# Expert passes of a graph network: the sums of two groups in one run of 48 products

## The chip, the cores and the metric

One core of a Trainium2 chip runs the whole program. The metric is the device time of one execution in microseconds (us), the median over the runs. The engines are named as in the profile: PE is TensorE (PEld its weight loads), DVE VectorE, ACT ScalarE, POOL GpSimd, SP SyncE.

## The reference, cut to what matters

Four graph layers follow one another on 6250 nodes and 106250 edges, which are sorted by their target. The change touches the second layer alone, a mixture of experts with three levels (N, H = 6250, 256):

```python
h = x @ W_in + b_in
for l in range(3):
    agg = segment_sum(h[src], dst, num_segments=N) / deg
    logits = concatenate([h, agg], -1) @ router_W[l] + router_b[l]
    vals, idx = top_k(logits, 2); gates = softmax(vals)
    gate_dense = zeros_like(logits).at[rows, idx].set(gates)
    weak = relu(einsum('nh,ehf->nef', agg, weak_W[l]) + weak_b[l])           # 4 experts
    sh = relu(einsum('nh,ehf->nef', agg, strong_W1[l]) + strong_b1[l])       # 4 experts
    strong = einsum('nef,efh->neh', sh, strong_W2[l]) + strong_b2[l]
    moe = einsum('ne,neh->nh', gate_dense, concatenate([weak, strong], 1))
    h = h + sigmoid(h @ conf_W[l] + conf_b[l]) * moe
return h @ W_out + b_out
```

## The kernel before

Each level is one pass over the edges (`edge_pass` with `width == H`), and the experts of a block of 128 nodes are computed in the same pass, between the sums of the edges.

**The edges.** 128 edges are a tile, four tiles a group (`GROUP`), four groups a turn of the ring (`RING` = 16 slots in SBUF). POOL fills a slot with an indirect DMA of the 128 source rows (L546); each row holds h cut into three bf16 parts, so a tile is 128 x 768 bf16. POOL may gather into slot k of the next turn once `tiles_done` says that the slot's products are made (L544). DVE writes one-hot matrices for eight tiles at a time (L622), PE makes six products of 64 columns per tile (L696) that add up a group's sums in a PSUM bank, 24 per group, and DVE adds the group's sums into `acc` at the group's window (L662 to L669). There are two such banks: the products of group n wait until group n-2 has been added (`added`), and the addition of group n waits for `tiles_done`. A pass has 208 groups. `tiles_done` rises by four with the last product of a group; POOL, DVE and PE's partners read it.

**The blocks.** A pass is written out as 49 steps (`STEP_GROUPS`: 6, then eleven times 4, 4, 4, 5, then 4, 4, 4, 3 groups). Each step also does one block of nodes. The block's work is cut into pieces with a due place from 0 to 15, which `over` spreads over the tiles of the step, on each engine in program order: first the tile's own work, then the pieces that are due. Before the change PE runs a group's 24 products at the group's fourth tile. In a step of four groups PE's order is:

```text
down2 down3 | h_t weak0 | G0 | logits weak1 up0 up1 | G1 | down0 up2 | G2 | down1 up3 | G3
```

`down2` and `down3` (L1159) belong to the block before (`late_pe`), `h_t` (L1175), `weak` (L1184), `logits` (L1210), `up` (L1198) and `down` to the block itself (`on_pe`). `agg` (L1097, DVE) is the first piece of a block: it reads `acc` after all sums of the step before, so it waits for the last addition; `weak0` waits for `agg`. `logits` waits for ACT's copy of `h_t` (L1056), `up1` for DVE's `biased0` (L1106), which waits for `weak0`. `down0` waits for `relu0` (ACT, L1082), which stands behind `relu_w1` (L1062), which waits for `biased1`. `down3` of the next step waits for `relu3` and `mix5` (L1087).

DVE's order in the same step is: one-hots, `agg`, `mix6`, `next_row` and its cuts, addition of G0, `biased0` and the routing, addition of G1, six mixes, one-hots, three mixes, addition of G2, `mix5`, addition of G3.

In a step of five groups the pieces lie a little further apart: PE's order is `down2 down3 | G0 | h_t weak0 logits weak1 | G1 | up0 up1 | G2 | down0 up2 down1 | G3 | up3 | G4`.

Of the kernel before, what the change touches and what calls it, by code (L numbers as in the profile page):

```python
# [7 lines left out]
D = 128  # L8
H = 256
# [5 lines left out]
GROUP = 4  # L15
WIN = 64
RING = 16
HALF = RING // 2
GROUPS = RING // GROUP
# [4 lines left out]
STEP_GROUPS = (6,) + PERIOD * PERIODS + (4, 4, 4, 3)  # L24
STEPS = len(STEP_GROUPS)
FIRST_GROUP = [sum(STEP_GROUPS[:i]) for i in range(STEPS + 1)]
assert FIRST_GROUP[STEPS] == TURNS * GROUPS
ROW = GROUP * P
SETS = -(-E // (ROW * P))
TCOLS = SETS * P * GROUP  # L30
# [4 lines left out]
SPARE = SPARE_BLOCK * P  # L35
# [32 lines left out]
ALU = mybir.AluOpType  # L68
# [82 lines left out]
def gnn_kernel(nc, t, out):  # L151
    ctx = ExitStack()
    with ctx:
# [8 lines left out]
        gathered = [ctx.enter_context(nc.semaphore(f"gathered{k}")) for k in range(RING)]  # L162
# [32 lines left out]
        acc = sb("acc", [P, 2, NPAD])  # L195
# [5 lines left out]
        win = sb("win", [1, GCOLS], I32)  # L201
# [225 lines left out]
        def edge_pass(table, width, work, edge_net=None, prologue=None):  # L427
# [11 lines left out]
            with ExitStack() as tmp:  # L439
# [24 lines left out]
                def programs(block, sems, loop):  # L464
# [143 lines left out]
                    @block.vector  # L608
                    def _(dve):
                        if loop == "blocks" and not edge_net:  # L610
                            first_round()

                        def one_hots(i, h):

                            dve.wait_ge(tiles_done, i * RING + HALF * (h + 1))
                            cols = rel[:, bass.ds(i * RING + h * HALF, HALF)].unsqueeze(2).to_broadcast([P, HALF, WIN])
                            places = iota_row[:, :].unsqueeze(1).to_broadcast([P, HALF, WIN])
                            if edge_net:
                                dve.wait_ge(sem[f"rel_loaded{h}"], i * 16 + 16)
                                nc.vector.tensor_scalar(onehot_t[:, h, :], relb[:, h, :], iota_col[0:WIN, 0:1], None,  # L620
                                                        ALU.is_equal)
                            nc.vector.tensor_tensor(onehot[:, h, :, :], places, cols, ALU.is_equal).then_inc(onehot_ready, 1)  # L622

                        def dots(i, g):

                            n = i * (2 * GROUPS) + 2 * g
                            k = g * GROUP
                            dve.wait_ge(sem["z_done"], i * GROUPS + (g + 1))
                            nc.vector.tensor_tensor(hidden[:, :, :], zt[:, g % 2, :, :], ring[:, k:k + GROUP, 0:D],
                                                    ALU.subtract).then_inc(sem["net_own"], 1)  # L630
                            dve.wait_ge(sem["net_own"], n + 1)
                            nc.vector.scalar_tensor_tensor(
                                out=hidden[:, :, :], in0=hidden[:, :, :], scalar=0.0,
                                in1=w2.unsqueeze(1).to_broadcast([P, GROUP, D]), op0=ALU.max,
                                op1=ALU.mult).then_inc(sem["net_own"], 1)
                            dve.wait_ge(sem["net_own"], n + 2)
                            nc.vector.tensor_reduce(dot[:, g % 2, :], hidden[:, :, :], AX.X,
                                                    ALU.add).then_inc(sem["dot_done"], 1)

                        def tile(i, k, ahead=True):  # L640
                            g, q = divmod(k, GROUP)
                            if edge_net and q == 0:

                                dve.wait_ge(sem["weight_done"], i * GROUPS + (g + 1))
                                dve.wait_ge(tiles_done, i * RING + GROUP * (g + 3))
                                j = g * GROUP % HALF
                                nc.vector.tensor_tensor(onehot_w[:, g % 2, :, :], onehot[:, g // 2, j:j + GROUP, :],  # L647
                                                        weight[:, g % 2, :].unsqueeze(2).to_broadcast([P, GROUP, WIN]),
                                                        ALU.mult).then_inc(sem["weighted"], 1)
                            if q == 0 and g % 2 == 0:  # L650

                                one_hots(i + g // 2, 1 - g // 2)
                            if q < GROUP - 1:
                                return
                            if edge_net and (ahead or g < GROUPS - 1):

                                dots(i + (g + 1) // GROUPS, (g + 1) % GROUPS)
                            if edge_net:
                                if i * GROUPS + g >= 1:
                                    add_sums(i * GROUPS + g - 1)  # L660
                                return
                            w = dve.value_load(win[0:1, bass.ds(i * GROUPS + g, 1)], min_val=0, max_val=SPARE)  # L662
                            dve.wait_ge(tiles_done, i * RING + (GROUP * (g + 1) + RING))

                            dve.wait_ge(added, i * GROUPS + (g + 2))
                            nc.vector.tensor_tensor(  # L666
                                acc[:, 0:n_sums, bass.ds(w, WIN)], acc[:, 0:n_sums, bass.ds(w, WIN)],
                                sums[:, g % 2, 0:n_sums * WIN].rearrange("p (a j) -> p a j", j=WIN),
                                ALU.add).then_inc(added, 1)  # L669

                        def add_sums(n):

                            w = dve.value_load(win[0:1, bass.ds(n, 1)], min_val=0, max_val=SPARE)
                            dve.wait_ge(sem["turned"], n + 1)
                            dve.wait_ge(added, n + 2)
                            nc.vector.tensor_tensor(acc[0:1, 1, bass.ds(w, WIN)], acc[0:1, 1, bass.ds(w, WIN)],
                                                    sums[0:1, n % 2, WIN:2 * WIN], ALU.add)
                            nc.vector.tensor_tensor(acc[:, 0, bass.ds(w, WIN)], acc[:, 0, bass.ds(w, WIN)],
                                                    sums[:, n % 2, 0:WIN], ALU.add).then_inc(added, 1)

                        if loop == "edges":
                            dve.sem_inc(added, 2)
                            one_hots(0, 0)
                        if edge_net:
                            if loop == "edges":
                                nc.vector.memset(ring[:, :, YH:YH + 1], 1.0)
                                dots(0, 0)
                            over(dve, tile, lambda i, k: tile(i, k, ahead=False), lambda: add_sums(LAST_GROUP))
                        else:
                            over(dve, tile)  # L690

                    @block.tensor
                    def _(pe):
                        def tile_sum(ap, lhs, rhs, first, last=False):

                            return nc.tensor.matmul(ap, lhs, rhs, start=first, stop=last, skip_group_check=True)  # L696
# [45 lines left out]

                        def tile(i, k):
                            g, q = divmod(k, GROUP)
                            if k % HALF == 0:
                                pe.wait_ge(onehot_ready, i * 2 + (k // HALF + 1))
                            if q == 0:

                                pe.wait_ge(added, i * GROUPS + (g + 1))
                            burst = width == H  # L750
                            if burst and q < GROUP - 1:
                                return
                            for j in range(k - q if burst else k, k + 1):
                                pe.wait_ge(gathered[j], i * 16 + 16)
                                hot = onehot[:, g // 2, j % HALF, :]
                                for a in range(width // D):
                                    for c in range(PARTS):
                                        lo = c * width + a * D
                                        last = tile_sum(sums[:, g % 2, a * WIN:(a + 1) * WIN], ring[:, j, lo:lo + D],
                                                        hot, j % GROUP == 0 and a == 0 and c == 0, j % GROUP == GROUP - 1)  # L760
                            if q == GROUP - 1:
                                last.then_inc(tiles_done, GROUP)

                        if loop == "edges":
                            pe.sem_inc(tiles_done, RING)
# [1900 lines left out]
```

## Time and profile before

| | us |
|---|---|
| median of three runs | 8308.41 (8306.09 to 8310.05) |
| the profiled execution | 8296.74 |
| its span, first to last instruction | 8294.9 |
| first start of a sum product of the expert passes, last start | 1084.2, 5499.2 |
| granted TensorE clock over the span | 0.846 |

Busy shares over the whole span: PE 82%, PEld 60%, DVE 48%, ACT 25%, POOL 40%. The clock has two levels, shown as 0.5 and 1.0 of 2.4 GHz; a figure between is a mean over time. In a timeline row the first number is the start in us, the second its length, and the brackets at the end give the idle time of that engine just before and what ended it by the profile. Rows that follow one another with one line and shape are merged (x24).

### The profile page before, as it was taken

Reading aid. Unit: us, or ns where it says so; the run is one execution under the profiler, and the core shown is the slowest. Engines: PE = TensorE matmul, PEld = TensorE weight load, DVE = VectorE, ACT = ScalarE, POOL = GpSimd, SP = SyncE. Lnnn points to the kernel's source line nnn. Section 1 sums busy time; section 2 is a strip of 40 time slices with the busy share of each in tenths; the row PEclk is TensorE's granted clock in tenths of the full one; section 3 lists DMA queues with packets and bytes.
Section 4 is the critical chain, followed back from the end, with each engine's and each line's share of the span. In section 5 each row is a group of like instructions: output and inputs, shape, how many; then the busy total and the mean of one; then the engine's idle time right before and its main releaser. Section 6 shows DMA issues by size and latency. Waiting matters only on the chain. (4 is left out here: it accounts for less than half of the span.)

```text
span 8294.9 us, 149947 instructions
## 1 busy us (share of the span) xinstructions
PE 6806.2 (82%) x51092; PEld 4987.8 (60%) x51092; DVE 3941.9 (48%) x11483; ACT 2108.0 (25%) x6166; POOL 3355.4 (40%) x3406
## 2 busy tenths in 40 slices
PE   3999858888886888888688888867677676989899
PEld 1555546777775776777577777755555553545455
DVE  7777634444443444444355554546666662112111
ACT  3555412222221222222233333322222221000000
POOL 0000055555554555555455555536666661000000
PEclk6999979999997999999899999985555557999999
DMA  5344355454544444455444444434444445656565
GB/s 149 110 147 117 124 151 143 141 143 142 146 138 138 139 141 137 140 145 142 134 141 141 137 139 138 138 89 124 127 125 128 125 125 186 198 171 196 175 203 162
DMA packets 714970, 1188.63 MB, mean 143 GB/s; under 512 B 258881, under 2 KB 512997, under 8 KB 712162
## 3 DMA queue, kind: packets, MB, share of 16 engines
q0 software_dynamic: 200640, 601.97, 26.2%
q1 hardware_dynamic: 466786, 447.42, 18.0%
q10 hardware_dynamic: 46784, 129.65, 4.4%
q8 instruction: 411, 6.73, 0.3%
q14 instruction: 349, 2.86, 0.1%
HBM read 993.57 MB, written 185.20 MB: 142 GB/s over the span
## 5 line engine op out<-in xcount | busy, mean ns | idle before, releaser
L546 POOL DMA_INDIRECT ring<-parts,src_idx x2496 | 2453.7, 983 | 1948.1 <-PE sums L696 749.9
L1198 PEld LDWEIGHTS hid<-agg,big 128*128 128x128 f32 x9408 | 1157.1, 197 | 124.6 <-issue 88.1
L1198 PE MATMUL hid<-agg,big 128*128 128x128 f32 x9408 | 1184.7, 281 | 45.8 <-issue 27.3
L2346 PE MATMUL agg_ps<-sheet,big 128*128 128x448 f16 x6174 | 1193.6, 353 | 34.7 <-DMA sheet<-adj 34.7
L1159 PE MATMUL y<-big,strong 128*128 128x256 f32 x4704 | 1143.2, 390 | 37.3 <-issue 27.9
L546 POOL DMA_INDIRECT ring<-rows_yh,src_idx x832 | 839.5, 1009 | 556.8 <-issue 326.3
L1159 PEld LDWEIGHTS y<-big,strong 128*128 128x128 f32 x4704 | 868.8, 192 | 155.7 <-issue 50.1
L666 DVE TENSOR_TENSOR acc<-acc,sums 128x128 f32 x624 | 180.0, 289 | 1634.4 <-DMA acc<-in_edge_type 1116.1
L2346 PEld LDWEIGHTS agg_ps<-sheet,big 128*128 128x128 bf16 x6174 | 605.0, 99 | 581.7 <-DMA sheet<-adj 37.4
L1082 ACT ACTIVATE strong<-hid,s_b 128x128 f32<-128x128 f32 x2352 | 668.2, 369 | 916.5 <-PE hid L1198 625.4
L696 PE MATMUL sums<-onehot,ring 128*128 128x64 bf16 x14976 | 627.7, 196 | 320.5 <-issue 254.5
L696 PEld LDWEIGHTS sums<-onehot,ring 128*128 128x128 bf16 x14976 | 570.0, 100 | 480.3 <-issue 440.6
L1184 PE MATMUL hid<-big,agg 128*128 128x512 f32 x1176 | 764.8, 784 | 68.0 <-DVE agg L1097 65.8
L739 PE MATMUL by_target<-ring,onehot_w 128*64 128x129 f32 x1664 | 409.1, 427 | 133.7 <-DVE onehot_w L647 105.8
L1087 DVE SCALAR_TENSOR_TENSOR row<-y,gate,row 128x256 f32<-128x256 f32 x588 | 282.8, 481 | 376.5 <-DMA adj<-big 278.7
L739 PEld LDWEIGHTS by_target<-ring,onehot_w 128*64 128x64 f32 x1664 | 328.4, 223 | 178.8 <-issue 176.3
L1931 PE MATMUL counts_ps<-hot_col,hot 128*128 128x392 bf16 (+3 forms) x1960 | 348.2, 299 | 101.2 <-DVE hot_col L1790 96.7
L1184 PEld LDWEIGHTS hid<-big,agg 128*128 128x128 f32 x1176 | 257.5, 242 | 278.2 <-issue 204.8
L1062 ACT ACTIVATE weak<-weak 128x512 f32<-128x512 f32 x294 | 184.9, 629 | 822.1 <-DVE weak L1106 685.3
L1762 POOL MEMSET acc<- 128x10976 f32 x1 | 9.2, 9245 | 940.1 <-PE deg_ps L1931 940.1
L2458 DVE SCALAR_TENSOR_TENSOR agg<-agg_ps,counts_hold,acc 128x448 f32<-128x448 f32 x42 | 28.7, 684 | 723.2 <-PE agg_ps L2346 723.2
L2402 POOL MEMSET acc<- 128x448 f32 (+1 forms) x28 | 13.4, 480 | 872.9 <-DVE agg L2458 872.9
(370 smaller groups left out, 8529.5 us busy)
## 6 DMA issues: line engine op xcount, KB each, us to landing
sheet<-adj SPq DMA_DIRECT2D x294, 784.0 KB, 4.2
ring<-parts,src_idx POOLq DMA_INDIRECT x2496
adj<-big ACTq DMA_DIRECT2D x7, 5488.0 KB
adj<-acc ACTq DMA_DIRECT2D x7, 5488.0 KB
hp<-parts SPq DMA_DIRECT2D x147, 192.0 KB
relb<-rel_rows ACTq DMA_DIRECT2D x106, 256.0 KB
parts<-cut SPq DMA_DIRECT2D x99, 192.0 KB, 3.2
h<-rows SPq DMA_DIRECT2D x147, 128.0 KB
```

The lines of the kernel that those rows point to most:

```text
L546: nc.gpsimd.indirect_dma_start(ring[:, k, 0:YH] if edge_net else ring[:, k, :], None, table, bass.IndirectOffsetOnAxis(ap=src_idx[:, i * R ...
L666: nc.vector.tensor_tensor(acc[:, 0:n_sums, bass.ds(w, WIN)], acc[:, 0:n_sums, bass.ds(w, WIN)], sums[:, g % 2, 0:n_sums * WIN].rearrange(" ...
L696: return nc.tensor.matmul(ap, lhs, rhs, start=first, stop=last, skip_group_check=True)
L739: last = nc.tensor.matmul(by_target[:, g % 2, 0:D + 1], onehot_w[:, g % 2, j, :], ring[:, g * GROUP + j, D:YH + 1], start=(j == 0), stop=( ...
L1062: m.done(f"relu_w{q}", nc.scalar.activation(both, both, ACT.Relu))
L1082: ins = nc.scalar.activation(s["strong"][:, e % 2, j, :], p["hid"][:, bank_at, j * P:(j + 1) * P], ACT.Relu, bias=self.w["s1_b"][:, e, j:j ...
L1087: m.done(name, nc.vector.scalar_tensor_tensor(out=out, in0=expert, scalar=self.b[0]["gate"][:, e:e + 1], in1=so_far, op0=ALU.mult, op1=ALU ...
L1159: ins = nc.tensor.matmul(y, s["strong"][:, e % 2, k, :], w["s2"][:, k, e, :], start=(k == 0), stop=(k == 3))
L1184: ins = nc.tensor.matmul(hid, s["agg"][:, k, :], w["weak"][:, k, 2 * q:2 * q + 2, :].rearrange("p e f -> p (e f)"), start=(k == 0), stop=( ...
L1198: ins = nc.tensor.matmul(p["hid"][:, bank_at, j * P:(j + 1) * P], w["s1"][:, k, e, j * P:(j + 1) * P], s["agg"][:, k, :], start=(k == 0), ...
L1931: return nc.tensor.matmul(ap, lhs, rhs, start=first, stop=last, skip_group_check=True)
L2346: last = nc.tensor.matmul(ps[:, g % 2, 0:HALF_COLS], now[:, b, c, :], sheet[:, k, s * HALF_COLS:(s + 1) * HALF_COLS], start=(b == 0 and c ...
```

## The change

In the expert passes the groups of a step are paired: (0, 1), (2, 3), and the last of an odd number alone. PE does nothing at the first group of a pair; at the last tile of the second it makes both groups' products, 48 in one run, each group with its own waits and its own rise of `tiles_done`. DVE does both additions at the same place. Where the second group of a pair is an even one, the one-hots that used to be made at its first tile are made behind the two additions. PE's order in a step of four groups is now `down2 down3 h_t weak0 logits weak1 up0 up1 | G0 G1 | down0 up2 down1 up3 | G2 G3`; in a step of five, `down2 down3 h_t weak0 logits weak1 | G0 G1 | up0 up1 down0 up2 down1 | G2 G3 | up3 | G4`.

```diff
+PAIRS = [tuple(range(FIRST_GROUP[i] + g, FIRST_GROUP[i] + min(g + 2, STEP_GROUPS[i])))
+         for i in range(STEPS) for g in range(0, STEP_GROUPS[i], 2)]
+PAIR_AT_END = {pair[-1]: pair for pair in PAIRS}
+SECOND = {pair[1] for pair in PAIRS if len(pair) > 1}
...
-                            if q == 0 and g % 2 == 0:
-
+                            n = i * GROUPS + g
+                            if g % 2 == 0 and q == (GROUP - 1 if not edge_net and n in SECOND else 0):
+                                if q:
+                                    pair_sums(n)
                                 one_hots(i + g // 2, 1 - g // 2)
+                                if q:
+                                    return
...
-                            w = dve.value_load(win[0:1, bass.ds(i * GROUPS + g, 1)], min_val=0, max_val=SPARE)
-                            dve.wait_ge(tiles_done, i * RING + (GROUP * (g + 1) + RING))
-
-                            dve.wait_ge(added, i * GROUPS + (g + 2))
-                            nc.vector.tensor_tensor(
-                                acc[:, 0:n_sums, bass.ds(w, WIN)], acc[:, 0:n_sums, bass.ds(w, WIN)],
-                                sums[:, g % 2, 0:n_sums * WIN].rearrange("p (a j) -> p a j", j=WIN),
-                                ALU.add).then_inc(added, 1)
+                            pair_sums(n)
+
+                        def pair_sums(end):
+
+
+                            for n in PAIR_AT_END.get(end, ()):
+                                w = dve.value_load(win[0:1, bass.ds(n, 1)], min_val=0, max_val=SPARE)
+                                dve.wait_ge(tiles_done, GROUP * (n + 1) + RING)
+
+                                dve.wait_ge(added, n + 2)
+                                nc.vector.tensor_tensor(
+                                    acc[:, 0:n_sums, bass.ds(w, WIN)], acc[:, 0:n_sums, bass.ds(w, WIN)],
+                                    sums[:, n % 2, 0:n_sums * WIN].rearrange("p (a j) -> p a j", j=WIN),
+                                    ALU.add).then_inc(added, 1)
...
-                            if k % HALF == 0:
-                                pe.wait_ge(onehot_ready, i * 2 + (k // HALF + 1))
-                            if q == 0:
-
-                                pe.wait_ge(added, i * GROUPS + (g + 1))
-                            burst = width == H
-                            if burst and q < GROUP - 1:
+                            if q < GROUP - 1:
                                 return
-                            for j in range(k - q if burst else k, k + 1):
-                                pe.wait_ge(gathered[j], i * 16 + 16)
+                            for n in PAIR_AT_END.get(i * GROUPS + g, ()):
+                                group_sums(n)
+
+                        def group_sums(n):
+
+
+                            pe.wait_ge(onehot_ready, n // 2 + 1)
+                            pe.wait_ge(added, n + 1)
+                            g = n % GROUPS
+                            for q in range(GROUP):
+                                j = g * GROUP + q
+                                pe.wait_ge(gathered[j], n // GROUPS * 16 + 16)
                                 hot = onehot[:, g // 2, j % HALF, :]
                                 for a in range(width // D):
                                     for c in range(PARTS):
                                         lo = c * width + a * D
-                                        last = tile_sum(sums[:, g % 2, a * WIN:(a + 1) * WIN], ring[:, j, lo:lo + D],
-                                                        hot, j % GROUP == 0 and a == 0 and c == 0, j % GROUP == GROUP - 1)
-                            if q == GROUP - 1:
-                                last.then_inc(tiles_done, GROUP)
+                                        last = tile_sum(sums[:, n % 2, a * WIN:(a + 1) * WIN], ring[:, j, lo:lo + D],
+                                                        hot, q == 0 and a == 0 and c == 0, q == GROUP - 1)
+                            last.then_inc(tiles_done, GROUP)
```

## Rows read from the trace of the kernel before

**Rows 1.** Windows, passes 1 and 3: length, busy time per engine, PE clock, DMA share.

```profile
1084.00:2498.00 1414.00, 1208.08 (x10645) 988.51 (x10646) 636.87 (x1889) 328.86 (x1057) 819.75 (x830) 0.91 0.51 146
4037.00:5500.00 1463.00, 1237.76 (x11043) 1016.82 (x11043) 714.93 (x2354) 497.61 (x1338) 799.15 (x823) 0.91 0.49 140
```

**Rows 2.** Page, costliest groups: count, busy us, mean ns, idle before, releaser.

```profile
L666 DVE TENSOR_TENSOR acc<-acc,sums 128x128 f32 x624 | 180.0, 289 | 1634.4 <-DMA acc<-in_edge_type 1116.1
L696 PE MATMUL sums<-onehot,ring 128*128 128x64 bf16 x14976 | 627.7, 196 | 320.5 <-issue 254.5
```

**Rows 3.** Timeline of PE, one step from its last-but-one group on.

```profile
1643.93 0.86 PE L696 MATMUL sums<-onehot,ring 128*128 128x64 bf16 x24
1644.63 3.70 PE L1159 MATMUL y<-big,strong 128*128 128x256 f32 x16
1648.17 0.50 PE L1175 MATMUL misc<-ident,hp 128*128 128x128 bf16 x6
1650.71 1.98 PE L1184 MATMUL hid<-big,agg 128*128 128x512 f32 x4 [2.04 <-DVE agg L1097]
...
1653.23 0.59 PE L1210 MATMUL misc<-router,ht 128*128 128x9 f32 x4
...
1654.12 1.96 PE L1184 MATMUL hid<-big,agg 128*128 128x512 f32 x4
1655.92 3.73 PE L1198 MATMUL hid<-agg,big 128*128 128x128 f32 x32
1659.49 0.86 PE L696 MATMUL sums<-onehot,ring 128*128 128x64 bf16 x24
```

**Rows 4.** Timeline of DVE, the additions around the same place.

```profile
1642.87 0.29 DVE L666 TENSOR_TENSOR acc<-acc,sums 128x128 f32 x1 [1.15 <-DMA acc<-in_edge_type]
...
1649.29 0.29 DVE L666 TENSOR_TENSOR acc<-acc,sums 128x128 f32 x1 [5.74 <-DMA acc<-in_edge_type]
...
1650.23 0.42 DVE L1097 TENSOR_TENSOR agg<-acc,rdeg 128x256 f32<-128x256 f32 x1
```

**Rows 5.** Timeline of POOL: first gathers of two runs of four in sequence.

```profile
1643.51 0.95 POOL L546 DMA_INDIRECT ring<-parts,src_idx  x1 [1.15 <-DMA acc<-in_edge_type]
...
1649.93 1.07 POOL L546 DMA_INDIRECT ring<-parts,src_idx  x1 [1.71 <-DMA acc<-in_edge_type]
```

**Rows 6.** Timeline of POOL: first gather of a run of eight, first of the next.

```profile
1704.80 1.07 POOL L546 DMA_INDIRECT ring<-parts,src_idx  x1 [1.62 <-PE sums L696]
...
1717.09 1.06 POOL L546 DMA_INDIRECT ring<-parts,src_idx  x1 [2.42 <-DMA acc<-in_edge_type]
```

**Rows 7.** Waits of POOL, 1100 to 5500: us in total, times, longest.

```profile
POOL ring L546 <- PE sums L696: 749.6, 243, 6.8
...
POOL ring L546 <- DMA acc<-in_edge_type: 441.5, 262, 3.7
```

**Rows 8.** Timeline of POOL and PE: a group's products late in a run of eight.

```profile
2149.30 0.95 POOL L546 DMA_INDIRECT ring<-parts,src_idx  x1 [2.15 <-DMA acc<-in_edge_type]
...
2149.37 0.86 PE L696 MATMUL sums<-onehot,ring 128*128 128x64 bf16 x24
...
2156.66 0.28 PE L696 MATMUL sums<-onehot,ring 128*128 128x64 bf16 x4
...
2160.69 0.72 PE L696 MATMUL sums<-onehot,ring 128*128 128x64 bf16 x16 [0.51 <-issue]
2161.22 2.06 PE L1198 MATMUL hid<-agg,big 128*128 128x128 f32 x8
```

**Rows 9.** Timeline of POOL, PE and ACT: `h_t` in a run of eight.

```profile
1730.25 1.06 POOL L546 DMA_INDIRECT ring<-parts,src_idx  x1 [1.63 <-DMA acc<-in_edge_type]
...
1733.96 0.50 PE L1175 MATMUL misc<-ident,hp 128*128 128x128 bf16 x6
...
1741.67 0.37 ACT L1056 COPY ht<-misc 128x256 f32<-128x256 f32 x1 [7.26 <-DMA h_in<-rows]
...
1742.10 1.02 PE L1210 MATMUL misc<-router,ht 128*128 128x9 f32 x4 [3.82 <-ACT ht L1056]
```

## The prediction

> **What bounds the kernel now.** I read the passes' windows first. Pass 1 takes 1414 us, of which PE is busy 1208 and idle 206: with 49 steps that is 28.9 us a step, 24.7 busy and 4.2 idle. Pass 3 has the same picture, 1463 with 225 idle; the granted clock is 0.91 in both, so part of the busy time is work at half speed [rows 1]. The groups of the page say what the change moves: 624 additions and 14976 products of 64 columns, 208 groups in each of three passes. DVE's 1634 us of idle time ahead of the additions costs nothing in itself, but it is put down to a DMA of long ago, so something else ends it [rows 2].
>
> The timeline of a clean step gives the work at full clock, from start to start: 16 `down` products 3.54 us, `h_t` and its copy's cover about 0.4, `logits` 0.89, one `weak` 1.80, the 32 products of two `up` 3.57, a group's sum 0.70 [rows 3]. A step of four groups is 32 `down` 7.1, `h_t` 0.4, two `weak` 3.6, `logits` 0.9, 64 `up` 7.1, four sums 2.8: 21.9, say 22.1 with the seams. So of 28.9 us 2.6 are half clock (24.7 less 22.1) and 4.2 idle.
>
> Then the waits. The group of 1643.93 ends at 1644.79, and DVE, which stands at its addition with nothing before it, adds at 1649.29 only, 4.5 us later. `agg` follows at 1650.23, and PE loses 2.04 us before `weak` [rows 3, 4]. In that time POOL issues four gathers: first at 1643.51, and the next run's first at 1649.93 [rows 5]. The addition comes when POOL has finished its run: **what PE reports while POOL issues gathers becomes visible late**, often only after the run. One run of four and the pause behind it takes 6.42 us (1649.93 less 1643.51); where two groups are ready, POOL issues eight in one run, 12.29 us from first to first [rows 6]. POOL waited for a group 505 times (243 and 262) for 624 groups, so some 119 groups joined a run already going [rows 7]. Four such cycles are 25.7 us a step: PE's chain and POOL's chain are both near the bound, and each stall feeds the other.
>
> **The change part by part.** Additions, products, one-hots and gathers are as many as before [rows 2]; the order alone changes.
>
> *POOL.* Both groups of a pair become ready 0.70 us apart, and nearly always before POOL's run has got going, so nearly every run is one of eight. A pair costs POOL 12.29 instead of 2 x 6.42 = 12.84 us: 0.55 us less, 104 pairs x 3 passes = 172 us if POOL's chain alone set the time. It is the lower bound of the change.
>
> *PE, behind the pair that ends a step.* `down2`, `down3` and `h_t` end about 4 us after the pair, `weak0` about 5.4. `weak0`'s report falls into the run of eight. A case shows what that means: run from 1730.25, `h_t` ends at 1734.46, 4.2 us into it, and ACT copies it at 1741.67, 11.4 us into it; PE's `logits` stand 3.82 us [rows 9]. Here `weak0` is late in the same way: `biased0` can't start before +11.4, `up1` not before +12.2. PE's own order is there at 5.4 + 0.9 + 1.8 + 1.8 = 9.9. Loss: 2.3 to 2.6 us. Before, additions of G0 stood ahead of `biased0` as well, and the loss was part of the 4.2.
>
> *PE, behind the pair in the middle.* `down0`, `up2`, `down1`, `up3` take 1.77 + 1.78 + 1.77 + 1.78 = 7.1 us, then G2 and G3 start 7.1 us into a run of eight. The rows hold the same place: run from 2149.30, 24 products start at 2156.66, 7.4 us into it. Four pass, then single ones, and 16 at once from 2160.69; the next work starts at 2161.22. 4.56 us for 0.70 [rows 8]. The first group of the pair meets this, the second comes at full pace: 3.9 us. Below, the loss is 0 if only the late report and not PE itself is slowed; above, 2 x 3.9. I take 3.9, which is a row's.
>
> *The half clock.* After that stretch eight `up` products take 2.06 us [rows 8], against 3.73 for 32 [rows 3]: half speed. There are two long stops a step now where there were up to four short ones. Between nothing and twice the present 2.6 us a step I take 1.9.
>
> The Trainium skill ("TensorE: Matmul & The Clock Gate", section "HAM oscillation — how this bites in real kernels") says that a pause which recurs in each round of a loop makes every round start at half clock. The trace agrees in the row just named; by the rule alone the loss would be the upper end, 5.2 us a step, and the sum 485 us higher.
>
> *DVE.* The second addition stands 1.15 + 0.29 us behind the first (the register load ahead of an addition is in the 1.15 [rows 4]), so `agg` moves by up to 1.4 us. The 3.54 us of `down` and `h_t` cover it [rows 3]; without them it is 1.4 x 147 steps = 206 us. The one-hots that move behind two additions, 0.7 us, have the 7 us of work between two pairs as cover.
>
> *ACT.* `logits` has no group ahead of it, but the 1.8 us of `weak0` cover ACT's copy of 0.37 [rows 9]; `relu0` comes behind `relu_w1` and `biased1`, which the late `biased0` moves to about +15, just where the middle pair ends: 0 to 0.6 us.
>
> *The gathers.* G0's slots come free some 6 us later than now and G2's 3.6. They are needed a step later, over 20 us, and filled in 5 to 10 us: nothing. The fifth group of a long step uses slots that G0 of the same step frees; 12 us of work lie between, four gathers take 5. Its own report falls 2.7 us into a run of eight and can hang until +11.4: up to 5 us in 11 steps a pass, which I leave to the upper end.
>
> **The sum.** A mean step: 22.1 work + 2.6 + 3.9 idle + 1.9 half clock = 30.5 us, against 28.9: 1.6 more, x 147 = 235 us. 8296.7 + 235 = 8532 for the profiled execution; the median of the runs lies 11.7 above that one: **8545 us**, 2.8% slower.
>
> **The rivals.**
>
> *POOL's chain is the bound, and fewer runs help: faster.* For it: 25.7 us a step at POOL against 22.1 at PE, and PE's 2.04 us before `weak` ends with POOL's run [rows 3 to 5]. Against it: the pass has 28.9 a step, so something beyond POOL's cycle costs 3.2. It gives 8308 - 172 = 8136 us. Chance 0.31.
>
> *`h_t` is caught too: slower by much.* In the forecast it ends about 4.0 us into the run; the case with 4.2 was held to 11.4 [rows 9]. If a slow pair delays `down2`, it is caught in every other step or more. Price: 3.8 us of stop and 1.2 of half clock behind it. It decides from an `h_t` that ends later than about 4.1 us into a run. In half of the steps: 5.0 x 73 = 367 on top, 8910 us. Chance 0.18.
>
> *Reports are not held by the run, the additions are merely late for another cause: no change.* The Trainium skill ("Perfetto Trace Analysis", section "Tensor Engine Instruction (MATMUL, LD_WEIGHTS)") has the semaphore update pushed when PSUM has acknowledged the writes, which would be at the group's end. The trace differs by 4.5 us [rows 4]. If reports were prompt after a pair, the order of the pieces would change nothing that PE waits for: 8308. Chance 0.08.
>
> The forecast has 0.43.
>
> **How the numbers follow.** Less than 0.2%, 17 us, can't be told from no change here. Faster: 0.31. Same: 0.08. Slower: 0.43 + 0.18 = 0.61. The range reaches from a little below the fast rival, 8120, to 8900, about where the second rival has half its weight; that leaves some 0.1 on either side. The forecast's own range, with the burst's loss from 2 to 5 us and the clock's from 1 to 3, is 8310 to 8850.
>
> **What would show it.** In the timeline of POOL nearly all runs have eight gathers, and its waits for groups fall from 505 to about 330. The first group of the middle pair takes over 4 us from its first product to its last, with single products about 0.7 us apart; the second takes 0.7. `up1` is released by `biased0` 12 us after the run's start. PE's idle share in the pass windows rises from 0.15 to above 0.2. The prediction is wrong if the products of a pair run through at 33 ns each although POOL is in a run of eight, if the additions follow a pair within half a us, or if PE's idle time in the pass falls. The granted clock of the windows tells how much of a difference is half clock: I expect 0.90 to 0.93.

## The result, and the profile of the changed kernel

The changed kernel takes 8754.7 us (8710.0 to 8771.7, four runs), the kernel before 8307.3 beside it: a ratio of 1.0528, with a 95% interval of 1.0492 to 1.0564. It is 447 us slower, where 238 were forecast. All ratios below are to the kernel before on the same chip, whose median moved between 8257 and 8311 us from chip to chip.

The windows of the three expert passes say where the loss lies. The rows that answer to those of before ([rows 1] for the first pass) are these, of the changed kernel. The columns are length, then busy time and count for PE, PE's weight loads, DVE, ACT and POOL, granted clock, DMA share and GB/s:

```profile
1084.00:2599.00 1515.00, 1224.26 (x10630) 1012.08 (x10631) 651.48 (x1889) 323.95 (x1057) 806.72 (x827) 0.89 0.47 135
2599.00:4163.00 1564.00, 1245.97 (x10777) 1030.12 (x10776) 667.03 (x1937) 330.60 (x1079) 811.38 (x832) 0.89 0.46 133
4163.00:5938.00 1775.00, 1350.74 (x11200) 1101.92 (x11199) 741.59 (x2403) 504.75 (x1360) 804.03 (x832) 0.86 0.41 118
```

and for passes 2 and 3 of the kernel before, from the last group of one pass to the last of the next:

```profile
2498.00:3983.00 1485.00, 1245.75 (x10774) 1017.71 (x10774) 654.09 (x1936) 334.70 (x1078) 822.55 (x832) 0.90 0.49 140
3983.00:5500.00 1517.00, 1263.09 (x11198) 1037.00 (x11197) 730.65 (x2401) 504.41 (x1360) 808.44 (x832) 0.91 0.49 138
```

Length less before's length: +101, +79, +258, in all 438 of the 455 us by which the profiled spans differ. The gain in PE's busy time is 16, 0 and 88, so the rest is idle PE: +85, +79 and +170. The first two passes lose what was forecast (1.6 us x 49 steps = 78 each), or a little more; the third loses more than three times as much. PE's idle share of the three is 0.19, 0.20 and 0.24.

**Inside a pass the loss is not spread over the steps.** These windows of the changed kernel are four steps in a row of pass 1, each up to the end of its last group. The first is a long step of five groups, the second the step behind it, and then come two ordinary ones:

```profile
1709.89:1742.96 33.07, 26.87 (x240) 22.11 (x240) 14.37 (x41) 6.19 (x21) 17.19 (x18) 0.86 0.44 124
1742.96:1780.63 37.67, 26.56 (x216) 20.50 (x216) 12.97 (x38) 7.20 (x24) 17.24 (x18) 0.86 0.42 119
1780.63:1808.68 28.05, 24.71 (x216) 20.75 (x216) 13.28 (x39) 6.84 (x23) 15.94 (x17) 0.93 0.49 140
1808.68:1836.37 27.69, 24.20 (x216) 20.62 (x216) 13.58 (x40) 6.68 (x22) 16.11 (x17) 0.93 0.49 141
```

The same four of the kernel before:

```profile
1670.49:1704.57 34.08, 28.57 (x239) 22.02 (x238) 13.21 (x40) 6.60 (x22) 18.67 (x20) 0.85 0.48 138
1704.57:1730.58 26.01, 23.59 (x216) 19.39 (x216) 13.57 (x41) 7.00 (x25) 15.98 (x17) 1.00 0.52 144
1730.58:1760.74 30.16, 25.37 (x216) 20.92 (x216) 13.56 (x40) 6.91 (x23) 16.59 (x17) 0.89 0.48 137
1760.74:1788.81 28.07, 24.63 (x215) 20.07 (x215) 13.20 (x39) 6.91 (x23) 15.50 (x16) 0.94 0.48 139
```

The two ordinary steps are together 2.5 us shorter in this example, the long one 1.0 shorter, and the step behind it is 11.7 us longer. Over all steps of passes 1 and 2, each from the end of the last group before it to the end of its own last, the 48 ordinary ones (four groups, and four in the step before) take 28.0 us on average (27.9 before), the 22 long ones 31.8 (33.2) and the 22 behind a long one 36.2 (27.1). The last kind loses 22 x 9.1 = 200 us; the long steps give 31 back. The timeline of the step behind the long one shows why. First PE and then DVE of the changed kernel (start, length, engine, line, operation, what went out and in, and in brackets the idle time before it):

```profile
1742.10 0.86 PE L712 MATMUL sums<-onehot,ring 128*128 128x64 bf16 x24
1742.80 3.70 PE L1178 MATMUL y<-big,strong 128*128 128x256 f32 x16
...
1752.79 3.78 PE L1203 MATMUL hid<-big,agg 128*128 128x512 f32 x4 [5.62 <-DVE agg L1116]
1758.40 0.61 PE L1229 MATMUL misc<-router,ht 128*128 128x9 f32 x4 [1.83 <-ACT ht L1075]
```

```profile
1740.65 0.29 DVE L682 TENSOR_TENSOR acc<-acc,sums 128x128 f32 x1 [0.54 <-PE sums L712]
...
1751.40 0.29 DVE L682 TENSOR_TENSOR acc<-acc,sums 128x128 f32 x1 [9.47 <-DMA acc<-in_edge_type]
1752.31 0.42 DVE L1116 TENSOR_TENSOR agg<-acc,rdeg 128x256 f32<-128x256 f32 x1 [0.62 <-DVE acc L682]
```

and POOL's run of eight under it, its first gather and the first of the next run:

```profile
1740.47 0.94 POOL L552 DMA_INDIRECT ring<-parts,src_idx  x1 [8.33 <-PE sums L712]
...
1752.05 0.94 POOL L552 DMA_INDIRECT ring<-parts,src_idx  x1 [1.88 <-DMA acc<-in_edge_type]
```

The long step's fifth group stands alone behind the pair and 16 `up` products. It ends at 1742.96, 2.5 us into a run of eight that the pair started. Its addition comes at 1751.40, 10.9 us into that run; `agg` waits for the addition, and PE's `weak` stands 5.62 us for `agg`. `logits` stand 1.83 more for ACT's copy of `h_t`, and the products behind these stops run at half clock (four `weak` in 3.78 us, 1.98 in [rows 3]).

**The ordinary step** has the forecast's slow group, though. It is G2, in the step's second pair (G2 G3), which the prediction and some expectations call the middle pair. PE of the changed kernel, this pair and the `down` products of the next step:

```profile
1676.56 0.42 PE L712 MATMUL sums<-onehot,ring 128*128 128x64 bf16 x9
...
1679.33 0.19 PE L712 MATMUL sums<-onehot,ring 128*128 128x64 bf16 x1 [1.22 <-issue]
1680.04 0.19 PE L712 MATMUL sums<-onehot,ring 128*128 128x64 bf16 x1 [0.52 <-issue]
1680.74 1.51 PE L712 MATMUL sums<-onehot,ring 128*128 128x64 bf16 x35 [0.52 <-issue]
1682.07 5.05 PE L1178 MATMUL y<-big,strong 128*128 128x256 f32 x16
```

Single products 0.7 us apart, 5.5 us for the pair's 48 instead of 1.4, then `down` at half speed for a while (5.05 us against 3.70 in [rows 3]). Over the 72 four-group steps of passes 1 and 2, G2 takes 4.9 us (median) where a group alone takes 0.86, and G3 1.35.

### The profile page after: what moved, and what is told of

Its sections match the earlier page's. It is cut to its first block and busy times, and to the rows that moved or that the text cites. A ratio compares the mean times of both kernels' runs of the same rounds, so it can differ in the third digit from the quotient of the medians.

```text
span 8749.9 us, 150208 instructions
## 1 busy us (share of the span) xinstructions
PE 6913.1 (79%) x51092; PEld 5088.9 (58%) x51092; DVE 3980.3 (45%) x11483; ACT 2099.1 (24%) x6166; POOL 3329.8 (38%) x3406
## 5 line engine op out<-in xcount | busy, mean ns | idle before, releaser
L552 POOL DMA_INDIRECT ring<-parts,src_idx x2496 | 2427.4, 972 | 2422.0 <-PE sums L712 1535.8
L1178 PE MATMUL y<-big,strong 128*128 128x256 f32 x4704 | 1281.7, 426 | 129.3 <-ACT strong L1101 74.8
L1217 PE MATMUL hid<-agg,big 128*128 128x128 f32 x9408 | 1163.7, 279 | 21.3 <-issue 21.2
L1178 PEld LDWEIGHTS y<-big,strong 128*128 128x128 f32 x4704 | 976.4, 216 | 289.7 <-ACT strong L1101 81.6
L712 PE MATMUL sums<-onehot,ring 128*128 128x64 bf16 x14976 | 651.0, 203 | 408.5 <-issue 337.2
L1203 PE MATMUL hid<-big,agg 128*128 128x512 f32 x1176 | 701.5, 727 | 120.6 <-DVE agg L1116 115.4
L1203 PEld LDWEIGHTS hid<-big,agg 128*128 128x128 f32 x1176 | 238.1, 225 | 311.6 <-issue 186.1
L1125 DVE TENSOR_TENSOR weak<-hid,weak_b 128x512 f32<-128x512 f32 x294 | 202.5, 689 | 446.3 <-PE hid L1203 200.0
L724 PE MATMUL zt<-ywin,onehot_t 64*128 64x128 bf16 x2496 | 345.4, 306 | 18.4 <-DMA ring<-rows_yh,src_idx 12.8
L2477 DVE SCALAR_TENSOR_TENSOR agg<-agg_ps,counts_hold,acc 128x448 f32<-128x448 f32 x42 | 28.7, 684 | 724.0 <-PE agg_ps L2365 724.0
```

The source lines that it names most:

```text
L552: nc.gpsimd.indirect_dma_start(ring[:, k, 0:YH] if edge_net else ring[:, k, :], None, table, bass.IndirectOffsetOnAxis(ap=src_idx[:, i * R ...
L724: last = nc.tensor.matmul(zt[:, g % 2, q, :], onehot_t[:, g // 2, (k % HALF) * P:(k % HALF + 1) * P], ywin[:, g, c * D:(c + 1) * D], start ...
L1125: m.done(f"biased{q}", nc.vector.tensor_tensor(s["weak"][:, 2 * q:2 * q + 2, :], p["hid"][:, q, :].rearrange("p (e f) -> p e f", f=H), sel ...
L1178: ins = nc.tensor.matmul(y, s["strong"][:, e % 2, k, :], w["s2"][:, k, e, :], start=(k == 0), stop=(k == 3))
L1203: ins = nc.tensor.matmul(hid, s["agg"][:, k, :], w["weak"][:, k, 2 * q:2 * q + 2, :].rearrange("p e f -> p (e f)"), start=(k == 0), stop=( ...
L1217: ins = nc.tensor.matmul(p["hid"][:, bank_at, j * P:(j + 1) * P], w["s1"][:, k, e, j * P:(j + 1) * P], s["agg"][:, k, :], start=(k == 0), ...
```

## The experiments

Twelve kernels ran. Each part starts with the edit.

**The fifth group.** Only the cuts of the long step change:

```diff
-PAIRS = [... for g in range(0, STEP_GROUPS[i], 2)]        # G0 G1 | G2 G3 | G4
+CUTS = {5: (0, 2, 3)}                                     # G0 G1 | G2 | G3 G4
+PAIRS = [... from each of CUTS.get(STEP_GROUPS[i], range(0, STEP_GROUPS[i], 2)) to the next]
```

> The fifth group of a long step is no longer alone behind a pair: the pairs of a five-group step are (G0 G1), G2, (G3 G4), so the pair stands at the step's end and G4's report is made together with G3's. The trace of the changed kernel shows 33 steps that follow a five-group step, mean 35.6, 36.7 and 38.7 us in the three passes, where the other four-group steps take 28, 28 and 34. Theory (G4's report falls some 2.5 us into a run of eight and hangs until its end, so the addition, agg and weak0 come late): these 33 steps fall to the others' length, 11 x (7.6 + 8.8 + 4.6) = 230 us less, about 8520. Rival (pairs cost in every step alike, the long step only shows where two slips add up): the time stays within 60 us of 8755. Second rival (the lone G2 now has a report of its own that is held in the same way): half is given back, 8640.

Measured: 8513.8 us, 1.0262 (1.0230 to 1.0295), against 8520 expected. Its pass windows:

```profile
1084.00:2504.00 1420.00, 1198.76 (x10635) 1004.45 (x10635) 651.46 (x1888) 323.79 (x1055) 812.07 (x828) 0.91 0.51 145
2504.00:3966.00 1462.00, 1223.17 (x10781) 1022.06 (x10776) 667.31 (x1936) 329.80 (x1080) 817.23 (x832) 0.90 0.50 142
3966.00:5699.00 1733.00, 1348.50 (x11203) 1110.23 (x11200) 739.26 (x2401) 507.45 (x1363) 808.71 (x832) 0.87 0.42 120
```

Passes 1 and 2 are back at the length of before (+6 and -23 us), although their steps still have pairs and slow middle groups. The third keeps +216.

**The third pass.** As that kernel, but the third pass takes its groups singly:

```diff
+single = bool(getattr(work, "last", None))
+pair_at_end = {n: (n,) for n in range(TURNS * GROUPS)} if single else PAIR_AT_END
```

> As the kernel with the long step's pairs at its end (8513.8 us), but the third expert pass takes its groups singly, as the kernel before does. In the trace of that kernel passes 1 and 2 take 1413 and 1404 us, against 1404 and 1429 before, and the third 1675 against 1462. Theory (in the third pass each step has more trips between PE and other engines, agg ahead of h_t, and the transposes and products of the output, and each of their reports hangs in the run of eight): the third pass falls back to about 1465, 8300 in all. Rival (the third pass suffers from its start or from what the passes before leave, not from its own pairs): it stays above 1600, 8450 or more.

Measured: 8235.8 us, 0.9975 (0.9965 to 0.9986); on the scale of the other chip 8311 x 0.9975 = 8290, against 8300 expected. The third pass takes 1513 us with 248 idle. So two edits, made one after the other, take the whole loss away: some 240 us (8754.7 less 8513.8) go with the long step's lone group and some 225 (8513.8 less 8290) with the pairs of the third pass. What is left is 0.25% faster than the kernel before.

**Without the gathers.** Both kernels with POOL's loop over turns cut to the first one in the expert passes, so that the first sixteen tiles are summed again and again:

```diff
-for i in turns(pool, 0, TURNS):
+for i in turns(pool, 0, TURNS if edge_net else 1):
...
-pe.wait_ge(gathered[j], n // GROUPS * 16 + 16)             # before the change: i * 16 + 16
+pe.wait_ge(gathered[j], 16)
```

> The changed kernel without the gathers of turns 1 to 51 in the three expert passes: only the first sixteen tiles are gathered and their rows are summed again and again, so POOL is idle in the passes; PE's order, waits on additions, one-hots and block work are as in the changed kernel. Theory (all that the pairs cost comes from POOL's runs of gathers, through held reports and a slowed PE): a step is PE's own work, 22.1 us or a little more, at the granted clock 1.0, about 147 x 6.5 = 950 us under the kernel before, near 7350, and the same as the kernel before with the same omission within 20 us. Rival (the order itself costs, the later agg and one-hots): over 100 us more than the kernel before with the same omission.

> The kernel before without the gathers of turns 1 to 51 in the three expert passes (first sixteen tiles summed again and again). Theory: the same as the changed kernel with this omission, near 7350, within 20 us. Rival: over 100 us less than that one. If it is far above 7350, PE's own chain and not POOL's runs holds most of a step's 28.9 us.

Measured: 7307.1 us with the changed order (0.8797, 0.8779 to 0.8814) and 7316.4 with the order of before (0.8807, 0.8790 to 0.8823). A stretch of 100 us in pass 1, first of the changed order, then of the other:

```profile
1500.00:1600.00 100.00, 100.00 (x989) 86.27 (x988) 61.69 (x179) 31.41 (x100) 0.00 (x0) 1.00 0.13 38
```

```profile
1500.00:1600.00 100.00, 100.00 (x997) 86.31 (x996) 59.98 (x174) 30.79 (x99) 0.00 (x0) 1.00 0.12 36
```

In this stretch PE never stops and has full clock. Pass 1 with its start takes 1085 us for 49 steps, 22.1 a step, the forecast's figure, and PE is idle for 19 to 22 us of it. So nearly all of PE's waits in both kernels, and nearly all of the half clock, need the gathers; the order of the groups makes 9 us of difference without them. What the omission can't tell is whether POOL's issuing or the DMA traffic that goes with it (a DMA share of 0.51 in pass 1, 0.13 here) does the harm. The mean traffic alone does not decide: the kernel with pauses below has a DMA share of 0.50 over the passes, the slower changed kernel 0.45.

**Runs of eight without pairs.** The kernel before, with one wait of POOL changed:

```diff
-pool.wait_ge(tiles_done, i * RING + (k + 1))
+pool.wait_ge(tiles_done, i * RING + (k // 8 * 8 + 8))      # expert passes
```

> The kernel before with one wait of POOL changed: in the expert passes POOL starts on a group's slots only when both groups of a half ring are summed, so every run has eight gathers, while PE, DVE and ACT keep their order with single groups. Theory (the loss is made by runs of eight, not by PE's products standing in pairs): slower than before by 2 to 6%, 8420 to 8750, with h_t, weak0 or a group wherever they fall between 3 and 11 us into a run. Rival (a run of eight harms only what stands right behind a pair in PE's order): within 1% of before, 8310 or a little less, since a pair of groups costs POOL 12.3 instead of 12.8 us.

Measured: 8941.8 us, 1.0811 (1.0793 to 1.0830): more than the theory's upper end. PE's order, additions and one-hots are those of before, so long runs of gathers alone make more than the changed kernel's loss; its pairs in PE's order are, if anything, the better fit to such runs. POOL also starts later here, but rows that come too late are not the cause: PE's waits for gathered rows in the passes are 86 us, before 64, of a loss of 676.

**Pauses in POOL.** If an unbroken run does the harm, a short stop should help. Behind each fourth gather POOL writes a small tile of its own, each memset waiting for the one before:

```diff
+if not edge_net and k % GROUP == GROUP - 1:
+    for r in range(PAUSES):                    # 2; also 1 and 3
+        pool.wait_ge(sem["paused"], (i * RING + k) // GROUP * PAUSES + r)
+        nc.gpsimd.memset(pause[:, :], 0.0).then_inc(sem["paused"], 1)   # 128 x 320
```

On the changed kernel, with two:

> The changed kernel with a pause of two small memsets (about 0.8 us together) on POOL behind each fourth gather of the expert passes: a run of eight becomes two of four with a short pause. Theory (PE's reports and PE's own issue recover when POOL stops issuing gathers for a moment): the first group of the middle pair takes 1 to 2 us instead of 5, G4's report comes after the first four gathers, and the time falls by 150 to 350 us, to 8400 to 8600. Rival (what counts is how many gathers POOL has issued or how much is in flight, not that the run is unbroken): the middle pair still takes 5 us and the pauses add to POOL's chain, 8755 or up to 100 more.

Measured: 8267.3 us, 0.9959 (0.9941 to 0.9976), 487 less than the changed kernel and less than the 8400 to 8600 expected. But the reason given is only half right. The products of a second pair of this kernel:

```profile
1752.66 1.18 PE L721 MATMUL sums<-onehot,ring 128*128 128x64 bf16 x35
...
1754.76 0.28 PE L721 MATMUL sums<-onehot,ring 128*128 128x64 bf16 x4 [0.50 <-issue]
1756.20 0.28 PE L721 MATMUL sums<-onehot,ring 128*128 128x64 bf16 x4 [1.16 <-issue]
```

The slow stretch has moved from the pair's first group to its second; it is not gone (G3 takes over 2 us in 63 of 72 steps, G2 in none). The waits of PE over the passes tell what is gone. Waited for, us in total, times, longest; first the changed kernel, then the one with pauses:

```profile
PE sums L712 <- issue: 337.2, 453, 5.1
PE hid L1203 <- DVE agg L1116: 115.4, 21, 12.0
PE misc L1229 <- ACT ht L1075: 92.6, 31, 10.1
PE misc L1194 <- DVE agg L1116: 91.7, 13, 10.8
PE y L1178 <- ACT strong L1101: 74.8, 23, 4.9
```

```profile
PE sums L721 <- issue: 330.1, 517, 2.8
...
PE hid L1212 <- DVE agg L1125: 44.8, 21, 4.6
PE misc L1238 <- ACT ht L1084: 39.2, 20, 4.3
...
PE misc L1203 <- DVE agg L1125: 15.5, 7, 6.1
```

Waits for the answer of another engine fall from 375 us in these rows to 100, and those for `strong` are no longer among the large ones; PE's slow issue in the sums stays (337 and 330). Idle PE falls by 348 us in the passes, and its busy time by 149, at a granted clock of 0.92 against 0.88.

With two memsets and the long step's pair at its end:

> The long step's pairs at its end, and POOL's pause of two memsets (0.8 us) behind each fourth gather. Alone the one gave 8514 and the other 8267. Theory (both take away the same thing in the long step, a report that hangs to the end of a run of eight; the pause takes the third pass's loss too): less than the sum, 40 to 80 us below 8267, because the steps behind a long one still take 30 us there against 26.5: about 8200. Rival (with pauses the place of the pairs is indifferent): 8267 within 20.

Measured: 8080.4 us, 0.9785 (0.9764 to 0.9807), better than expected (8200 is 0.987). With one memset in place of two, else as the last:

> As the kernel with the long step's pairs at its end and pauses, but a pause of one memset (about 0.4 us) instead of two. Theory (any stop lets the held reports through): as with two, or 20 to 50 us less, because a four costs POOL 0.4 us less: 8170 to 8200. Rival (the stop must be long enough for what waits): part of the loss comes back, the middle pair takes over 2 us and the third pass over 1500: 8300.

Measured: 8333.8 us, 1.0100 (1.0075 to 1.0124). That is the rival's side: one stop of 0.4 us takes part of the loss only (1.0262 without a stop, 0.9785 with two). From the second pass's last group to the third's it takes 1610 us, against 1446 with two.

With two memsets, the long step's pair at its end and the third pass in single groups:

> Pairs with the long step's pair at its end in passes 1 and 2, single groups in the third, and the pause of two memsets behind each fourth gather. Passes of 1343 and 1345 us were measured with pairs and pauses, 1318 and 1323 with single groups and pauses; the third takes 1391 with pairs and 1418 single. Theory (the three passes add up): 8080 + 27 = about 8105 on the chip where those gave 8080 and 8058, 0.981 of before. Rival (the order makes a pass faster or slower than its own pairs say): over 30 us from that.

Measured: 8093.7 us, 0.9798 (0.9781 to 0.9814), as expected (0.981). With the long step's pair at its end, pairs in all passes, and the pause between the two fours of a pair only:

> As the kernel with pauses and the long step's pair at its end (0.9785 of before), but POOL pauses only between the two fours of a pair, not behind the second, where it mostly waits for PE anyway. Theory (only an unbroken run of eight costs, a pause at its end gives nothing): the same as with all pauses, or up to 40 us less where POOL goes straight on: 0.974 to 0.979. Rival (the pause behind the second four lets reports through also): 0.985 or more.

Measured: 8161.1 us, 0.9873 (0.9856 to 0.9889): the rival's figure. The stop behind the pair's second four counts too.

On the kernel before, whose groups are single:

> The kernel before with POOL's pause of two memsets (0.8 us) behind each fourth gather. It has 114 runs of eight in the passes, with 3.2 us of idle PE in each against 0.4 in a run of four. Theory (unbroken runs cost): the runs of eight lose most of that, some 250 us, while runs of four pay up to 0.8 where POOL's chain holds the step: 8100 to 8250. Rival (before's bound is POOL's chain, 4 x 6.42 a step; each pause adds to it): 4 x 0.4 to 0.8 more in a step, 8400 to 8700.

Measured: 8057.9 us, 0.9757 (0.9733 to 0.9780); on the scale of the other chip 8311 x 0.9757 = 8109, at the theory's lower bound. With three memsets:

> The kernel before with a pause of three memsets (1.2 us) behind each fourth gather. One memset (0.4) gave little in the paired kernel, two (0.8) gave most. Theory (a stop has to be long enough for what PE holds back; beyond that it only adds to POOL's chain): with the need met by two, 0.4 us x 4 a step more on POOL, slower than with two: 0.980 to 0.995 of before. Rival (what PE holds back is not all out after two): faster than 0.9757 of before.

Measured: 8037.6 us, 0.9723 (0.9706 to 0.9739): the rival's side, though the two intervals touch. It is the fastest of all, faster than both kernels. But the passes tell it apart: 1351, 1399 and 1417 us, with two memsets 1327, 1378 and 1475. In the first two the third memset costs 24 and 21 us, as the theory had it; all that it gains is in the third pass. Its four gathers and pause take 6.57 us from first to first, as these two rows of POOL say:

```profile
1705.17 1.22 POOL L550 DMA_INDIRECT ring<-parts,src_idx  x1 [0.36 <-issue]
...
1711.74 1.08 POOL L550 DMA_INDIRECT ring<-parts,src_idx  x1 [0.36 <-issue]
```

208 x 6.57 = 1367 us, about the length of a pass (1351 for the first): POOL's chain is now near the bound. PE's waits say the same, where gathered rows take the first place:

```profile
PE sums L705 <- DMA ring<-parts,src_idx: 312.3, 309, 10.7
PE misc L1184 <- DVE agg L1106: 55.8, 34, 3.6
PE sums L705 <- issue: 49.0, 90, 2.1
```

## Why the prediction was right in sign and short in size

*What bounds the kernel: shown.* PE's own work is 22.1 us a step; the remaining 6.8 need POOL's gathers (the pair of runs without them). The rival in which POOL's chain is the bound and fewer runs help is refuted by the kernel with runs of eight alone, 8% slower. The rival in which no report is held is refuted by the addition that comes 8.4 us behind its group.

*Nearly all runs have eight: right.* POOL's waits for groups fall from 505 to 320 (288 and 32 in the passes), against 330 forecast.

*The late `biased0`, 2.6 us a step: wrong, it costs nothing.* PE's waits in the passes have no row for `up1` behind `biased0` any more (14 waits, 17.6 us before). In an ordinary step of passes 1 and 2 `h_t` ends 5.5 us into a run of eight (from 1654.43) and is copied 0.3 us later, and `biased0` follows 8.0 us into the run, where 11.4 was forecast. PE, ACT and DVE:

```profile
1659.40 0.50 PE L1194 MATMUL misc<-ident,hp 128*128 128x128 bf16 x6
```

```profile
1660.20 0.37 ACT L1075 COPY ht<-misc 128x256 f32<-128x256 f32 x1 [3.57 <-PE misc L1194]
```

```profile
1662.43 0.69 DVE L1125 TENSOR_TENSOR weak<-hid,weak_b 128x512 f32<-128x512 f32 x1 [0.53 <-PE hid L1203]
```

The forecast took over [rows 9]: held from 4.1 us on. In the kernel before that was nearly a rule: of 52 `h_t` that ended 4 us or more into a run of eight, ACT waited over 2 us for 50. With pairs it is 16 of 89 in passes 1 and 2, and 26 of 33 in the third. Why some reports in the second half of a run get through these runs do not settle.

*The additions behind a pair: a sign of being wrong, and it came.* The prediction called itself wrong if the additions follow a pair within half a us. In the four-group steps of passes 1 and 2 the last addition starts 0.2 us (median) behind the end of the step's last group, and within half a us in 59 of 72; before it was 3.1 us. Here the group ends at 1780.63:

```profile
1780.83 0.29 DVE L682 TENSOR_TENSOR acc<-acc,sums 128x128 f32 x1 [0.53 <-PE sums L712]
```

So PE's wait for `agg`, 0.7 us in a mean ordinary step before, is gone from the ordinary steps of these passes and stands behind the long ones (4.0 and 4.3 us a step there).

*The slow first group of the second pair, 3.9 us: right.* It costs 4.1 us in the step shown (5.5 less 1.4), and an ordinary step of passes 1 and 2 has 3.5 us of idle PE, 3.2 of them in the sums. With 22.1 of work and 2.4 lost to half clock that gives the 28.0 measured. The forecast had 30.5, and the term that failed is the 2.6 for `biased0`: without it the sum is 27.9. That is no loss, for ordinary steps took 27.9 before, with 3.0 of idle PE (1.6 in the sums, the rest mostly at `agg` and `logits`) and 2.8 lost to half clock; the forecast's 28.9 was the mean with the long steps in it. With the lone fifth group gone, pairs cost passes 1 and 2 nothing.

*The fifth group, left to the upper end with up to 5 us in 11 steps: this is the term that was mis-sized.* Its report falls 2.5 us into the run and hangs to 10.9, as the prediction's own sentence had it (2.7 and 11.4). The price is 11.7 us in the step shown: 5.6 of stop at `weak` and 1.8 at `logits`, more at half clock, and a run that begins late behind them. Moving the group took out 241 us. That passes 1 and 2 lost what the sum gave is luck: a term that was not there stood in for one that was left out.

*The third pass, not treated apart: the missing 180 us* (258 less 78). There `h_t` stands behind `agg` in PE's order and each step has further trips between PE and ACT (its own work is larger too: 1149 us without the gathers, against 1085 for pass 1). In this step POOL's run starts at 5053.15; PE first, then ACT:

```profile
5058.83 0.50 PE L1194 MATMUL misc<-ident,hp 128*128 128x128 bf16 x6
...
5063.72 0.80 PE L1229 MATMUL misc<-router,ht 128*128 128x9 f32 x4 [2.62 <-issue]
```

```profile
5063.29 0.37 ACT L1075 COPY ht<-misc 128x256 f32<-128x256 f32 x1 [5.08 <-DMA h_in<-rows]
```

`h_t` ends 6.2 us into the run and is copied 4.0 us later; in 26 of the 49 steps of this pass ACT waited over 2 us for it in that way. That is the second rival, `h_t` caught, in one pass only; its price of 5.0 us for such a step is near the 5.5 by which the ordinary steps of this pass grew (28.7 to 34.2). That pairs make the third pass's loss is shown by the kernel that takes them out; that this particular report carries it is read from the trace and was not tried by itself.

*Half clock, 1.9 us a step in place of 2.6: too small.* In pass 1 PE is busy for 25.0 us a step, 2.9 over its work (before 2.6); pass 2 has the busy time of before, and the third has 1.8 a step more (88 / 49). The granted clocks of the windows, 0.89, 0.89 and 0.86, lie under the 0.90 to 0.93 expected. In the two ordinary steps above it is 0.93, before 0.89 and 0.94: with 0.5 and 1.0 as its levels, 0.93 over 28 us is some 4 us at half clock in each step, by this estimate. The rule of the Trainium skill ("TensorE: Matmul & The Clock Gate", section "HAM oscillation — how this bites in real kernels") has each round of a loop start at half clock when a pause comes back in every round. The trace agrees in so far as none of 96 steps of passes 1 and 2 has a granted clock of 1.00, where 25 had it before, the one shown above among them; but the upper end that the prediction drew from it, 5.2 us a step, did not come.

The range held because it was drawn for `h_t` caught in half of the steps. What happened is of that kind and about that size, `h_t` in the third pass and the fifth group's report behind each long step, but not in the steps that the prediction meant; there, too, it had luck.

## What to carry to other kernels

Where one engine issues many indirect gathers in a row, what other engines report and issue meanwhile is late, so look at how long the unbroken runs are before the order of the others is tuned; a stop of 0.8 to 1.2 us behind each four gathers brought 2.4 to 2.8% here, where the best order of the groups alone brought 0.25%. Price an irregular step (the fifth group, the last layer) by itself, not as a tail of the mean: two such cases held nearly all of this loss. A stall that is new in a step has to be set against the stalls that the old step had, and a rule that the old trace shows 50 times in 52 need not outlive the change of order: here it did not.

## What the runs showed of the hardware

The length of the stop matters: behind four gathers no stop gave 1.0262, 0.4 us of memset 1.0100 and 0.8 us 0.9785, with the same order of groups. With single groups 0.8 gave 0.9757 and 1.2 gave 0.9723. The gathers' harm has two parts that can be told apart: late reports, which a stop of 0.8 us mostly cures (375 to 100 us of waits), and PE issuing single products 0.7 us apart. Two memsets leave the second in the paired kernel (337 and 330 us); with single groups it goes from 254 us without a pause to 126 with two and 49 with three, but there PE waits 312 us for gathered rows (83 with two), which may hide part of it. Whether the gathers' issue or their traffic holds the reports is open. Each memset of 128 x 320 took 0.37 to 0.38 us, and four gathers with three of them 6.57 us, little more than the 6.42 that a run of four and its wait took before [rows 5].
